# Moving one elementwise sum of a recurrent stage from VectorE to GpSimd, with a new instruction order

## The chip, the cores and the metric

One core of a Trainium2 chip runs the whole program. The time is the device time of one launch in microseconds; of several runs the median counts. The engines of the core that matter here are PE (TensorE, matmuls), ScalarE (ACT), VectorE (DVE) and GpSimd (POOL). Each has its own instruction stream and they meet through semaphores.

## What is computed

The reference is a decoder of twelve blocks on 8192 tokens (128 sequences of 64) of width 128, each block followed by a residual sum and a layer norm. The change lies in the seventh block, a four-layer recurrent block (RWKV). Cut to what matters:

```python
def wkv_scan(k, v, time_decay, time_first):
    w, u = -jnp.exp(time_decay), time_first
    def step(carry, kv):
        num, den, mx = carry
        kt, vt = kv
        max_out = jnp.maximum(mx, kt + u)
        e1, e2 = jnp.exp(mx - max_out), jnp.exp(kt + u - max_out)
        out = (e1 * num + e2 * vt) / (e1 * den + e2)
        ...                                # num, den, mx decayed by w and updated
for l in range(n_layer):                   # 4
    h = layer_norm(x, ln1_w[l]); prev = time_shift(h)
    k, v, r = ...                          # three projections of mixes of h and prev; r through a sigmoid
    x = x + (r * wkv_scan(k, v, time_decay[l], time_first[l])) @ tm_o_w[l].T
    h = layer_norm(x, ln2_w[l]); prev = time_shift(h)
    vv = jnp.square(jax.nn.relu(mix_k(h, prev) @ cm_k_w[l].T)) @ cm_v_w[l].T
    x = x + jax.nn.sigmoid(mix_r(h, prev) @ cm_r_w[l].T) * vv
```

## The kernel before

`rwkv` (from L2121) holds the block. The width of 128 lies on the partitions, tokens along the free axis. The tokens go in 16 tiles of 512 (8 sequences of 64), and each of the four layers passes over the 16 tiles, so there are 64 turns, numbered m. All instructions are written out, and one turn spreads over five to six turn lengths, so that several turns are in work at once. There is one buffer for nearly every intermediate; a step of turn m therefore also waits for the reader of turn m-1.

The steps of a turn are small functions of m, one list for each engine, and each has a due time in the list (in us, on the engine's own scale). `interleaved` (L168; `staggered`, L162, for GpSimd) sorts all steps of all turns by m * 17.9 + due time. The sorted list is the order of the engine's instructions; the due time has no other effect, and an engine runs its list in order, waiting where a semaphore is not yet there. Sixteen end tiles (the block's last layer norm: variance1, end_sum, end_variance2 and their partners) are sorted in behind the last turns with a scale of their own.

The way of a turn, with engines:
- normal1 (VectorE, L2525) makes the first normed tile; half_mixed_k, half_mixed_r (ScalarE) with mix_key, mix_r (VectorE, L2536, L2530) mix it with its shift; keys, values, receptance (PE) project.
- running_max (VectorE, a scan), exponents_ab (two instructions, L2559, L2560), exponent_g (L2568) and clamp_g (L2573) make exponents; exp_ab (L2351) and exp_g (ScalarE) take them. weighted, scan_den (L2586), scan_num (L2593) (VectorE) give the two sums over time, `den` and `num`.
- GpSimd adds the denominator: `dn[1:] = ex0[1:] + den[:-1]` (L2453). VectorE makes `gv = ex0 * v` (bonus, L2601) and then the numerator, in place, `gv[1:] += num[:-1]` (L2606). ScalarE takes the logarithm of the denominator (ln_denominator, L2361); denominator_r (GpSimd, L2458) adds to it ln(1 + exp(-r)), which clamp_r (VectorE) and exp_r, ln_r (ScalarE) have made; reciprocal (ScalarE, L2365) exponentiates, and the quotient (GpSimd, L2463) multiplies it to `gv`. output (PE, L2234) projects.
- residual1 (VectorE, L2610), square2 (ScalarE, L2371), variance2 (PE, L2238), rstd2 (ScalarE), normal2 (GpSimd, L2470) make the second normed tile, mix_k, mix_r2 (VectorE) with half_mixed and half_mixed_r2 (ScalarE) mix it.
- hidden (PE, two halves of 4 matmuls, L2248), rectified (ScalarE, L2399, both halves), squared (first half on ScalarE, L2403; second half on VectorE, L2626), contract (PE, two halves, L2263); receptance2 (PE), clamp_rr (VectorE), exp_rr, ln_rr, sigmoid_rr (ScalarE), gated (VectorE, L2637), centred (PE, L2268), residual2 (VectorE, L2641).

The inputs of bonus, clamp_r, clamp_rr, running_max, exponent_g, exponents_ab's second, weighted, residual1, squared, gated and residual2 include a PSUM bank (`ps`). normal1, mix_key, mix_r, mix_k, mix_r2, clamp_g, exponents_ab's first, scan_den, scan_num and the numerator read SBUF only.

Of the kernel before, what the change touches and what calls it, by code (L numbers as in the profile page):

```python
# [21 lines left out]
ALU = mybir.AluOpType  # L22
# [2098 lines left out]
def rwkv(nc, k, d, ahead=()):  # L2121
# [6 lines left out]
    with ExitStack() as ctx:  # L2128
# [67 lines left out]
        def _(pe):  # L2196
# [88 lines left out]
            def end_variance2(m):  # L2285
# [4 lines left out]
                else:  # L2290
# [1 line left out]
                pe.matmul(ps[:, 4, :], avg[:], rmix[:], start=True, stop=True).then_inc(evar2, 1)  # L2292

            interleaved((0, TURNS, 0, PERIOD, (
                            (1.6, variance1), (24.4, keys), (26.8, values), (32.6, receptance), (45.5, output),
                            (50.4, variance2), (62.5, lambda m: hidden(m, 0)), (60.3, receptance2),
                            (66.3, lambda m: hidden(m, 1)), (71.1, lambda m: contract(m, 0)),
                            (71.2, lambda m: contract(m, 1)), (77.2, centred))),
                        (TURNS, NT, END, END_PERIOD, ((6.3, variance1), (17.8, end_sum), (21.5, end_variance2))))

        @block.scalar
        def _(act):
# [123 lines left out]
            def end_rstd2(m):  # L2426
# [4 lines left out]
                else:  # L2431
# [4 lines left out]
                act.activation(tokens(mm[:]), tokens(mm[:]), ACT.Exp, scale=-0.5).then_inc(ers2, 1)  # L2436

            interleaved((0, TURNS, 0, PERIOD, (
                            (-24.4, square1), (10.7, half_mixed_r), (6.6, half_mixed_k), (-3.5, rstd1), (25.7, exp_r), (27.4, ln_r),
                            (28.2, ln_denominator), (17.3, exp_ab), (17.0, exp_g), (31.8, reciprocal),  # L2440
                            (37.2, square2), (40.3, rstd2), (44.3, half_mixed), (42.7, half_mixed_r2), (52.3, lambda m: rectified(m, 0)), (55.6, squared),
                            (55.8, lambda m: rectified(m, 1)),
                            (57.0, exp_rr), (59.6, ln_rr), (60.1, sigmoid_rr))),
                        (TURNS, NT, END, END_PERIOD, ((-10.7, square1), (-1.6, rstd1), (7.8, end_square2), (13.2, end_rstd2))))

        @block.gpsimd
        def _(pool):
            def denominator(m):
                pool.wait_ge(g_ready, m + 1)
                pool.wait_ge(den_ready, m + 1)  # L2450
                if m:
                    pool.wait_ge(ln_low, m)
                pool.tensor_tensor(flat(dn[:])[:, :, 1:S], ex[:, 0, :, 1:S], den[:, :, 0:S - 1], ALU.add).then_inc(low, 1)  # L2453

            def denominator_r(m):
                pool.wait_ge(ln_low, m + 1)
                pool.wait_ge(er_ready, m + 1)
                pool.tensor_tensor(tokens(dl[:]), er[:], tokens(dl[:]), ALU.add).then_inc(low_r, 1)  # L2458

            def quotient(m):  # L2460
                pool.wait_ge(rec, m + 1)
                pool.wait_ge(top, m + 1)
                pool.tensor_tensor(gv[:], gv[:], tokens(dl[:]), ALU.mult).then_inc(wkv, 1)  # L2463

            def normal2(m):
                pool.wait_ge(rs2, m + 1)
                if m:
                    pool.wait_ge(mixed, m)
                    pool.wait_ge(rmixed2, m)
                pool.tensor_tensor(hp2[:, :, 1:S1], flat(xw[:, at(m)[1]]), flat(rsb[:]), ALU.mult).then_inc(h2, 1)  # L2470

            pool.wait_ge(w_steps, 1)
            staggered(TURNS, PERIOD, (17.6, denominator), (21.7, denominator_r), (32.9, quotient), (38.8, normal2))

        @block.vector
        def _(dve):
# [166 lines left out]
            def end_close(m):  # L2643
# [3 lines left out]
                dve.tensor_tensor(xres[:, e * CT:(e + 1) * CT], ps[:, 2 + e % 2, :], tokens(mm[:]), ALU.mult).then_inc(eclosed, 1)  # L2647

            interleaved((0, TURNS, 0, PERIOD, (
                            (13.0, normal1), (21.7, mix_r), (14.9, mix_key), (31.4, clamp_r), (21.4, running_max), (24.1, exponents_ab),  # L2650
                            (22.4, exponent_g), (22.8, clamp_g), (29.2, weighted), (29.2, scan_den), (29.3, scan_num),
                            (31.1, bonus), (32.0, numerator), (46.5, residual1), (53.1, mix_k), (51.3, mix_r2), (65.6, squared), 
                            (63.2, clamp_rr),
                            (68.4, gated), (72.4, residual2))),
                        (1, NL - 1, PERIOD, PERIOD, ((-16.9, prepare),)),
                        (TURNS, NT, END, END_PERIOD, ((9.8, normal1), (26.1, end_close))))
# [1340 lines left out]
```

## Time and profile before

| | us |
|---|---|
| median of 3 runs | 4742.58 (4739.36 to 4744.38) |
| profiled execution, its own time | 4733.29 |
| its span | 4731.5 |
| of that the recurrent stage, from its first to its last instruction | about 1859 to 2924 |

Over the whole span PE is busy 91%, VectorE 72%, ScalarE 66%, GpSimd 40%. Those shares mix twelve stages with different limits; only the recurrent stage is touched, so it is read alone. Views used: busy time of each engine in a window, and timelines, in which a row is one instruction, or several merged ones, with its start and its duration in us. Durations of instructions that follow one another overlap by up to 0.1 us (0.16 for PE), so the cost of an instruction in a full engine is the distance from its start to the next start. An idle time before an instruction stands in brackets with what ended it.

### The profile page before, as it was taken

The page shows a single profiled execution, that of the slowest core. Times are in us where ns is not written, and L with a number is a line of the kernel's source. Part 1 is how long each engine was busy: PE and PEld are TensorE (multiplying, and loading weights), DVE is VectorE, ACT ScalarE, POOL GpSimd, SP SyncE. Part 2 cuts the span into 40 slices and gives each one's busy share as a digit, 9 for nine tenths or more (in the row PEclk, how much of TensorE's full clock was granted, in tenths as well). Part 3 has the DMA queues.
Part 4 walks back from the last instruction along what each step waited for, and adds up shares of the span by engine and source line. Part 5 has one row for each costly group of instructions (what it writes and reads, how often), then busy time and mean ns, then how long its engine had stood idle before and what let it go on. Part 6 is the DMA issues. An engine that isn't in the chain of part 4 may idle for free. (4 is left out here: it accounts for less than half of the span.)

```text
span 4731.5 us, 101446 instructions
## 1 busy us (share of the span) xinstructions
PE 4322.8 (91%) x37343; PEld 2844.9 (60%) x37343; DVE 3410.2 (72%) x5307; ACT 3131.8 (66%) x5627; POOL 1869.5 (40%) x2204
## 2 busy tenths in 40 slices
PE   8989889899979996999999998789979989999888
PEld 6767556556767774344444444566657767777565
DVE  8978777467764335999999994743359966666748
ACT  6878777466774335899999997742358844444356
POOL 4444344114416771343444430057724412222328
PEclk9999989899989998999999999899989999999999
DMA  3000000000021113000000001211130000000110
GB/s 108 3 2 3 2 1 1 1 1 15 2 61 43 52 52 115 1 1 1 1 1 1 1 1 39 93 40 52 52 100 3 2 2 2 2 2 1 58 56 37
DMA packets 123884, 119.28 MB, mean 25 GB/s; under 512 B 19472, under 2 KB 103952, under 8 KB 122640
## 3 DMA queue, kind: packets, MB, share of 16 engines
q1 hardware_dynamic: 106000, 77.11, 5.3%
q0 software_dynamic: 17408, 35.69, 2.6%
q8 instruction: 315, 5.16, 0.5%
q14 instruction: 161, 1.32, 0.1%
HBM read 82.34 MB, written 30.41 MB: 24 GB/s over the span
## 5 line engine op out<-in xcount | busy, mean ns | idle before, releaser
L1759 POOL DMA_INDIRECT L_ffn_xg<-L_ffn_xrows,L_ffn_take x272 | 264.1, 971 | 282.1 <-DVE L_ffn_take L2054 199.9
L1823 PEld LDWEIGHTS L_ffn_ps<-L_ffn_early_down,L_ffn_mT 128*128 128x128 f32 x1904 | 247.4, 191 | 105.2 <-issue 78.9
L2945 POOL TENSOR_TENSOR L_xattn_E<-L_xattn_E,L_xattn_rz 128x1024 f32<-128x1024 f32 x64 | 123.8, 1935 | 471.7 <-DVE L_xattn_rz L3165 471.7
L1765 POOL DMA_INDIRECT L_ffn_yrows<-L_ffn_yo,L_ffn_put x272 | 269.1, 989 | 99.2 <-issue 55.2
L2453 POOL TENSOR_TENSOR L_attn_dn<-L_attn_ex,L_attn_den 128x504 f32<-128x504 f32 x64 | 130.5, 2040 | 385.4 <-issue 293.0
L1803 PE MATMUL L_ffn_ps<-L_ffn_up,L_ffn_xT 128*128 x544 | 259.6, 559 | 19.8 <-issue 8.3
L1823 PE MATMUL L_ffn_ps<-L_ffn_early_down,L_ffn_mT 128*128 x1904 | 258.9, 276 | 2.4 <-DVE L_ffn_yo L2084 1.3
L2248 PE MATMUL L_attn_ps<-L_attn_mix,L_attn_wck 128*128 128x512 f32 x512 | 243.5, 598 | 0.0
L1913 ACT ACTIVATE L_ffn_mT<-L_ffn_ps 128x512 f32<-128x512 f32 x136 | 81.2, 597 | 236.8 <-PE L_ffn_ps L1812 236.8
L2263 PE MATMUL L_attn_ps<-L_attn_rl,L_attn_wcv 128*128 128x512 f32 x512 | 230.2, 592 | 0.0
L2073 DVE TENSOR_TENSOR L_ffn_m<-L_ffn_b,L_ffn_ps 128x512 f32<-128x512 f32 x136 | 93.6, 688 | 188.3 <-PE L_ffn_ps L1803 188.3
L2069 DVE TENSOR_TENSOR L_ffn_m<-L_ffn_sg,L_ffn_ps 128x352 f32<-128x352 f32 x136 | 70.9, 521 | 213.3 <-ACT L_ffn_sg L1903 213.3
L334 POOL TENSOR_TENSOR L_attn_Kbd<-L_attn_Kt,main_head_of_row 128x1024 f32<-128x1024 f32 x64 | 121.2, 1894 | 253.4 <-issue 244.8
L750 POOL TENSOR_TENSOR L_xattn_Kbd<-L_xattn_Kt,main_head_of_row 128x1024 f32<-128x1024 f32 x64 | 121.2, 1894 | 238.9 <-issue 233.3
L988 DVE TENSOR_REDUCE L_xattn_mx<-L_xattn_ps 128x16 f32<-128x1024 f32 x128 | 156.2, 1220 | 69.9 <-PE L_xattn_ps L812 69.9
L1095 POOL TENSOR_SCALAR L_ffn_aq<-L_ffn_aq,L_ffn_qinv 128x512 f32<-128x512 f32 x64 | 127.0, 1999 | 168.5 <-ACT L_ffn_aq L1245 168.5
L565 DVE TENSOR_TENSOR L_attn_ps<-L_attn_ps,L_attn_bias 128x512 f32<-128x512 f32 x256 | 165.0, 690 | 17.7 <-PE L_attn_ps L398 17.7
L2248 PEld LDWEIGHTS L_attn_ps<-L_attn_mix,L_attn_wck 128*128 128x128 f32 x512 | 92.8, 191 | 130.6 <-issue 130.0
L2263 PEld LDWEIGHTS L_attn_ps<-L_attn_rl,L_attn_wcv 128*128 128x128 f32 x512 | 97.0, 190 | 122.7 <-issue 93.3
L2458 POOL TENSOR_TENSOR L_attn_dl<-L_attn_er,L_attn_dl 128x512 f32<-128x512 f32 x64 | 81.6, 1275 | 209.1 <-ACT L_attn_dl L2361 209.1
L1903 ACT ACTIVATE L_ffn_sg<-L_ffn_ps 128x352 f32<-128x352 f32 x136 | 63.1, 464 | 146.8 <-PE L_ffn_ps L1805 146.8
L824 PE MATMUL L_xattn_ps<-main_ident,L_xattn_E 128*128 128x128 f32 x1024 | 145.5, 281 | 15.5 <-ACT L_xattn_Qt L875 10.3
(619 smaller groups left out, 13439.7 us busy)
## 6 DMA issues: line engine op xcount, KB each, us to landing
L_ffn_row_hot<-L_ffn_yrows SPq DMA_DIRECT2D x32, 256.0 KB, 2.9
L_ffn_col_hot<-L_ffn_yrows SPq DMA_DIRECT2D x32, 256.0 KB, 3.4
L_ffn_w<-in_L_ffn_e_W SPq DMA_DIRECT2D x32, 256.0 KB, 4.7
L_ffn_xrows<-L_ffn_xtok SPq DMA_DIRECT2D x42, 192.0 KB, 2.1
L_ffn_xg<-L_ffn_xrows,L_ffn_take POOLq DMA_INDIRECT x272, 2.5
L_ffn_yrows<-L_ffn_yo,L_ffn_put POOLq DMA_INDIRECT x272, 2.3
main_x<-in_xT SPq DMA_DIRECT2D x8, 512.0 KB, 7.6
main_ctx<-in_ctxT SPq DMA_DIRECT2D x4, 1024.0 KB, 11.5
```

Of the source, the lines that this page charges most:

```text
L565: b = dve.tensor_tensor(scores if in_place else E[t % 2][:, 8 * at:8 * at + 8, :].rearrange("p (a h) k -> p a (h k)", a=2), scores, bias_s ...
L824: m = pe.transpose(to[:, j * P:(j + 1) * P], E[t % 2][:, row:row + 2, :], k["ident"][:])
L988: dve.tensor_reduce(mx[t % 2][:, 16 * half:16 * half + 16], score_rows(half), AX, ALU.max) \
L1095: m = pool.tensor_scalar(aq[u][:, j, :], aq[u][:, j, :], ROUND, qinv[u][:, 1, j:j + 1], ALU.subtract, ALU.mult)
L1759: pool.indirect_dma_start(xg[t % RING][:], None, xrows, bass.IndirectOffsetOnAxis(ap=take[:, t:t + 1], axis=0)) \
L1765: pool.indirect_dma_start(yrows, bass.IndirectOffsetOnAxis(ap=put[:, t:t + 1], axis=0), yo[t % RING][:], None).then_inc(scattered[t % RING ...
L1803: g = pe.matmul(ps[u][:, 0, 0:F], xT[u][:], up[:, bass.ds(at, F)], start=True, stop=True)
L1823: g = pe.matmul(ps[1][:, 3, 0:P], mT[u][0:rows[a], a * P:(a + 1) * P], down[a][:, bass.ds(at, P)], start=(a == 0), stop=(a == FT - 1))
L2248: r = pe.matmul(ps[:, 5 + a % 2, :], wck[:, at(m)[0], a * P:(a + 1) * P], mix[:], start=True, stop=True)
L2263: r = pe.matmul(ps[:, 7, :], wcv[:, at(m)[0], a, :], rl[:, a, :], start=(a == 0), stop=(a == FT - 1))
L2453: pool.tensor_tensor(flat(dn[:])[:, :, 1:S], ex[:, 0, :, 1:S], den[:, :, 0:S - 1], ALU.add).then_inc(low, 1)
L2945: pool.tensor_tensor(E[u][:, j], E[u][:, j], rz[u][:, j].rearrange("p (a o) -> p a o", o=1).to_broadcast([P, 8, P]), ALU.mult).then_inc(no ...
```

## The change

The numerator's sum is taken from VectorE's list and stands as a fifth step in GpSimd's, with the same two waits (for bonus and for scan_num) and the same semaphore at its end, which the quotient and the next turn's scan_num wait for. Beside that every list has new due times: the steps, tiles, buffers and waits are the same, their order on each engine is another.

```diff
 @block.tensor
-  (1.6, variance1), (24.4, keys), (26.8, values), (32.6, receptance), (45.5, output),
-  (50.4, variance2), (62.5, hidden 0), (60.3, receptance2), (66.3, hidden 1), (71.1, contract 0),
-  (71.2, contract 1), (77.2, centred)
-  end: (6.3, variance1), (17.8, end_sum), (21.5, end_variance2)
+  (-4.1, variance1), (15.7, keys), (18.4, values), (22.3, receptance), (39.6, output),
+  (44.8, variance2), (54.9, hidden 0), (54.2, receptance2), (60.2, hidden 1), (63.6, contract 0),
+  (65.1, contract 1), (70.0, centred)
+  end: (-1.7, variance1), (11.9, end_sum), (14.7, end_variance2)
 @block.scalar
-  (-24.4, square1), (10.7, half_mixed_r), (6.6, half_mixed_k), (-3.5, rstd1), (25.7, exp_r), (27.4, ln_r),
-  (28.2, ln_denominator), (17.3, exp_ab), (17.0, exp_g), (31.8, reciprocal), (37.2, square2), (40.3, rstd2),
-  (44.3, half_mixed), (42.7, half_mixed_r2), (52.3, rectified 0), (55.6, squared), (55.8, rectified 1),
-  (57.0, exp_rr), (59.6, ln_rr), (60.1, sigmoid_rr)
+  (-21.7, square1), (13.2, half_mixed_r), (5.9, half_mixed_k), (-6.4, rstd1), (26.1, exp_r), (26.2, ln_r),
+  (24.1, ln_denominator), (16.4, exp_ab), (16.9, exp_g), (30.2, reciprocal), (37.0, square2), (39.2, rstd2),
+  (44.3, half_mixed), (42.1, half_mixed_r2), (52.5, rectified 0), (53.7, squared), (56.8, rectified 1),
+  (56.0, exp_rr), (59.1, ln_rr), (59.9, sigmoid_rr)
   ...
 @block.gpsimd
+def numerator(m):
+    pool.wait_ge(gv_ready, m + 1)
+    pool.wait_ge(num_ready, m + 1)
+    pool.tensor_tensor(flat(gv[:])[:, :, 1:S], flat(gv[:])[:, :, 1:S], num[:, :, 0:S - 1], ALU.add).then_inc(top, 1)
-staggered(TURNS, PERIOD, (17.6, denominator), (21.7, denominator_r), (32.9, quotient), (38.8, normal2))
+staggered(TURNS, PERIOD, (28.1, numerator), (19.2, denominator), (30.1, denominator_r), (34.9, quotient), (39.3, normal2))
 @block.vector
-def numerator(m):
-    dve.wait_ge(gv_ready, m + 1)
-    dve.wait_ge(num_ready, m + 1)
-    dve.tensor_tensor(flat(gv[:])[:, :, 1:S], flat(gv[:])[:, :, 1:S], num[:, :, 0:S - 1], ALU.add).then_inc(top, 1)
-  (13.0, normal1), (21.7, mix_r), (14.9, mix_key), (31.4, clamp_r), (21.4, running_max), (24.1, exponents_ab),
-  (22.4, exponent_g), (22.8, clamp_g), (29.2, weighted), (29.2, scan_den), (29.3, scan_num),
-  (31.1, bonus), (32.0, numerator), (46.5, residual1), (53.1, mix_k), (51.3, mix_r2), (65.6, squared),
-  (63.2, clamp_rr), (68.4, gated), (72.4, residual2)
+  (14.5, normal1), (24.0, mix_r), (15.6, mix_key), (32.7, clamp_r), (21.0, running_max), (22.7, exponents_ab),
+  (23.0, exponent_g), (24.7, clamp_g), (27.7, weighted), (28.8, scan_den), (31.7, scan_num),
+  (33.1, bonus), (46.4, residual1), (57.9, mix_k), (55.5, mix_r2), (67.7, squared),
+  (62.1, clamp_rr), (73.2, gated), (75.7, residual2)
   ...
```

The end groups of ScalarE and VectorE and the due time of prepare (the scaling of a layer's weights, VectorE) move by up to 3.2 as well.

## Rows read from the trace of the kernel before

**Rows 1.** Windows of the stage: busy us of each engine and (instructions).

```profile
core 0: us, PE busy (x) PEld busy (x) DVE busy (x) ACT busy (x) POOL busy (x), PEclk, DMA share, GB/s
...
2240.00:2360.00 120.00, 119.85 (x270) 49.06 (x269) 119.72 (x167) 112.30 (x175) 49.31 (x32) 1.00 0.00 1
```

**Rows 2.** Timeline of VectorE, one turn: start, duration, engine, line, tiles.

```profile
2399.84 1.20 DVE L2593 TENSOR_TENSOR_SCAN L_attn_num<-L_attn_ex,L_attn_bv 128x512 f32<-128x512 f32 x1
2400.96 1.20 DVE L2626 TENSOR_TENSOR L_attn_rl<-L_attn_rl,L_attn_ps 128x1024 f32<-128x1024 f32 x1
2402.07 0.69 DVE L2525 TENSOR_TENSOR L_attn_hp<-L_attn_xw,L_attn_rsa 128x512 f32<-128x512 f32 x1
...
2403.87 0.68 DVE L2606 TENSOR_TENSOR L_attn_gv<-L_attn_gv,L_attn_num 128x504 f32<-128x504 f32 x1
2404.46 0.68 DVE L2637 TENSOR_TENSOR L_attn_er<-L_attn_er,L_attn_ps 128x512 f32<-128x512 f32 x1
...
2409.42 0.73 DVE L2568 SCALAR_TENSOR_TENSOR L_attn_ex<-L_attn_ps,L_attn_col,L_attn_mm 128x504 f32<-128x504 f32 x1
2410.19 0.72 DVE L2573 TENSOR_SCALAR L_attn_ex<-L_attn_ex 128x504 f32<-128x504 f32 x1
2410.84 0.73 DVE L2559 SCALAR_TENSOR_TENSOR L_attn_ex<-L_attn_mm,L_attn_rate 128x504 f32<-128x504 f32 x1
2411.49 0.67 DVE L2560 TENSOR_TENSOR L_attn_ex<-L_attn_ps,L_attn_mm 128x504 f32<-128x504 f32 x1
...
2417.24 0.69 DVE L2525 TENSOR_TENSOR L_attn_hp<-L_attn_xw,L_attn_rsa 128x512 f32<-128x512 f32 x1
```

**Rows 3.** Timeline of PE, the same turn (xN: matmuls merged into one row).

```profile
2400.73 3.60 PE L2263 MATMUL L_attn_ps<-L_attn_rl,L_attn_wcv 128*128 128x512 f32 x8
2404.16 1.02 PE L2201 MATMUL L_attn_ps<-L_attn_sqa,main_avg 128*128 128x512 f32 x2
...
2412.20 1.88 PE L2248 MATMUL L_attn_ps<-L_attn_mix,L_attn_wck 128*128 128x512 f32 x4
```

**Rows 4.** Timeline of ScalarE, the same turn ([idle before, and who ended it]).

```profile
2408.43 0.63 ACT L2365 ACTIVATE L_attn_dl<-L_attn_dl 128x512 f32<-128x512 f32 x1 [0.25 <-POOL L_attn_dl L2458]
...
2412.20 1.04 ACT L2351 ACTIVATE L_attn_ex<-L_attn_ex 128x1008 f32<-128x1008 f32 x1 [0.47 <-DVE L_attn_ex L2560]
...
2414.87 1.00 ACT L2399 ACTIVATE L_attn_rl<-L_attn_ps 128x1024 f32<-128x1024 f32 x1
```

**Rows 5.** Timeline of VectorE, first turns of the stage.

```profile
1878.34 0.42 DVE L2573 TENSOR_SCALAR L_attn_ex<-L_attn_ex 128x504 f32<-128x504 f32 x1
...
1883.97 1.68 DVE L2525 TENSOR_TENSOR L_attn_hp<-main_x,L_attn_rsa 128x512 f32<-128x512 f32 x1
1885.57 0.68 DVE L2601 TENSOR_TENSOR L_attn_gv<-L_attn_ex,L_attn_ps 128x512 f32<-128x512 f32 x1
...
1898.91 1.68 DVE L2525 TENSOR_TENSOR L_attn_hp<-main_x,L_attn_rsa 128x512 f32<-128x512 f32 x1
```

**Rows 6.** Timeline of GpSimd, first turns of the stage.

```profile
1883.12 1.98 POOL L2453 TENSOR_TENSOR L_attn_dn<-L_attn_ex,L_attn_den 128x504 f32<-128x504 f32 x1 [92.36 <-DVE L_attn_den L2586]
...
1900.01 1.71 POOL L2470 TENSOR_TENSOR L_attn_hp<-L_attn_xw,L_attn_rsb 128x512 f32<-128x512 f32 x1
```

**Rows 7.** Timeline of GpSimd, one steady turn.

```profile
2400.06 2.04 POOL L2453 TENSOR_TENSOR L_attn_dn<-L_attn_ex,L_attn_den 128x504 f32<-128x504 f32 x1 [4.59 <-issue]
2402.55 1.35 POOL L2470 TENSOR_TENSOR L_attn_hp<-L_attn_xw,L_attn_rsb 128x512 f32<-128x512 f32 x1 [0.44 <-ACT L_attn_rsb L2379]
2407.13 1.28 POOL L2458 TENSOR_TENSOR L_attn_dl<-L_attn_er,L_attn_dl 128x512 f32<-128x512 f32 x1 [3.23 <-ACT L_attn_dl L2361]
2409.14 1.49 POOL L2463 TENSOR_TENSOR L_attn_gv<-L_attn_gv,L_attn_dl 128x512 f32<-128x512 f32 x1 [0.74 <-ACT L_attn_dl L2365]
```

**Rows 8.** One line's instructions (L2453, the denominator): duration ns min/median/max.

```profile
L2453 POOL TENSOR_TENSOR L_attn_dn<-L_attn_ex,L_attn_den x64: 1980/2042/2048, 1883.1 to 2840.7; 128x504 f32<-128x504 f32 x64
```

**Rows 9.** Timeline of VectorE, its first idle entry after the steady turns.

```profile
2846.75 0.69 DVE L2637 TENSOR_TENSOR L_attn_er<-L_attn_er,L_attn_ps 128x512 f32<-128x512 f32 x1 [1.27 <-PE L_attn_ps L2263]
```

More of the change, by code:

```diff
@@ L2294, in _ @@
             interleaved((0, TURNS, 0, PERIOD, (
-                            (1.6, variance1), (24.4, keys), (26.8, values), (32.6, receptance), (45.5, output),
[L2296 to L2299, printed above, removed]
+                            (-4.1, variance1), (15.7, keys), (18.4, values), (22.3, receptance), (39.6, output),
+                            (44.8, variance2), (54.9, lambda m: hidden(m, 0)), (54.2, receptance2),
+                            (60.2, lambda m: hidden(m, 1)), (63.6, lambda m: contract(m, 0)),
+                            (65.1, lambda m: contract(m, 1)), (70.0, centred))),
+                        (TURNS, NT, END, END_PERIOD, ((-1.7, variance1), (11.9, end_sum), (14.7, end_variance2))))
         @block.scalar
@@ L2438, in _ @@
             interleaved((0, TURNS, 0, PERIOD, (
-                            (-24.4, square1), (10.7, half_mixed_r), (6.6, half_mixed_k), (-3.5, rstd1), (25.7, exp_r), (27.4, ln_r),
[L2440 to L2444, printed above, removed]
+                            (-21.7, square1), (13.2, half_mixed_r), (5.9, half_mixed_k), (-6.4, rstd1), (26.1, exp_r), (26.2, ln_r),
+                            (24.1, ln_denominator), (16.4, exp_ab), (16.9, exp_g), (30.2, reciprocal),
+                            (37.0, square2), (39.2, rstd2), (44.3, half_mixed), (42.1, half_mixed_r2), (52.5, lambda m: rectified(m, 0)), (53.7, squared),
+                            (56.8, lambda m: rectified(m, 1)),
+                            (56.0, exp_rr), (59.1, ln_rr), (59.9, sigmoid_rr))),
+                        (TURNS, NT, END, END_PERIOD, ((-12.6, square1), (-2.2, rstd1), (7.8, end_square2), (12.9, end_rstd2))))
         @block.gpsimd
@@ L2649, in _ @@
             interleaved((0, TURNS, 0, PERIOD, (
-                            (13.0, normal1), (21.7, mix_r), (14.9, mix_key), (31.4, clamp_r), (21.4, running_max), (24.1, exponents_ab),
-                            (22.4, exponent_g), (22.8, clamp_g), (29.2, weighted), (29.2, scan_den), (29.3, scan_num),
-                            (31.1, bonus), (32.0, numerator), (46.5, residual1), (53.1, mix_k), (51.3, mix_r2), (65.6, squared),
[L2653 to L2656, printed above, removed]
+                            (14.5, normal1), (24.0, mix_r), (15.6, mix_key), (32.7, clamp_r), (21.0, running_max), (22.7, exponents_ab),
+                            (23.0, exponent_g), (24.7, clamp_g), (27.7, weighted), (28.8, scan_den), (31.7, scan_num),
+                            (33.1, bonus), (46.4, residual1), (57.9, mix_k), (55.5, mix_r2), (67.7, squared),
+                            (62.1, clamp_rr),
+                            (73.2, gated), (75.7, residual2))),
+                        (1, NL - 1, PERIOD, PERIOD, ((-20.1, prepare),)),
+                        (TURNS, NT, END, END_PERIOD, ((10.2, normal1), (25.1, end_close))))
 def padded_attention(nc, k, d, col, early, ahead):
```

## The prediction, made before the changed kernel was run

> **What bounds the kernel now.** I read the windows by stage first. In the recurrent stage (1859 to 2924 us) VectorE is busy 119.7 of every 120 us, PE 119.85, ScalarE 112.3, GpSimd 49.3 [rows 1]. Busy times of back-to-back instructions overlap a little, so two engines seem full; the timelines tell them apart. VectorE's has no idle entry in a whole turn: each instruction starts when the one before lets it, and a turn, from normal1 to normal1, is 2417.24 - 2402.07 = 15.17 us [rows 2]. PE starts the eight matmuls of contract, back to back, in 2404.16 - 2400.73 = 3.43 us, 0.429 each [rows 3]. A turn has 34 of them (keys, receptance, output, variance1, variance2, receptance2, centred 2 each; values, both halves of hidden, both of contract 4 each; 270 in 120 us = 7.91 turns [rows 1]). So PE needs 34 x 0.429 = 14.59 and is starved for 0.58 a turn. ScalarE idles too, before reciprocal and exp_ab [rows 4]. VectorE sets the pace, and PE stands 0.58 behind it: no change to VectorE can give more than 0.58 a turn.
>
> The third view is GpSimd's timeline beside VectorE's, in the first turns, where they collide. normal1, with two inputs in SBUF, takes 0.69 in the steady turns and 1.68 at 1883.97 and 1898.91 [rows 2, 5], where GpSimd's sum was running [rows 6]: it finished 0.55 after GpSimd's end at 1885.10. GpSimd's normal2 at 1900.01, behind a normal1 that was already waiting, took 1.71, against 1.35 in a steady turn [rows 6, 7]. VectorE's instructions with an input in PSUM (bonus, gated, squared) show no such thing. So a GpSimd instruction and a VectorE instruction that reads only SBUF exclude one another, and who has started finishes first.
> The Trainium skill says this in SBUF — State Buffer, section "Who interferes with whom": the pair of ports is an exclusive lock between GpSimd and a VectorE instruction with two SBUF inputs or in a two-port mode, and issue order decides. By that rule, the trace agrees. It is the rule that speaks against this change, since it moves work onto the engine that blocks VectorE.
>
> **Removed from VectorE.** 64 numerators, each worth 2404.46 - 2403.87 = 0.59 [rows 2]. The new order also parts clamp_g from exponent_g, which it reads: exponent_g takes 0.77 to the next start where the same form at 2410.84 takes 0.65 (the next is at 2411.49), so 0.12 [rows 2]. And clamp_g now overlaps GpSimd's quotient and takes 0.72, where it took 0.42 with GpSimd idle (1878.34) [rows 2, 5, 7]: 0.30 goes if the quotient lies elsewhere. Bare VectorE turn: 15.17 - 0.59 - 0.12 - 0.30 = 14.16.
>
> **Added to GpSimd.** The trace has no numerator there. From below: the denominator's sum, same shape, takes 2.04, but starts at 2400.06 while scan_num (SBUF only, from 2399.84) runs, and squared, the next on VectorE, starts at 2400.96; 0.90 would be waiting and 1.14 work [rows 2, 7]. denominator_r, with 512 contiguous elements, takes 1.28 alone [rows 7]. From above: 2.04, if the denominator's time is all its own. I take 1.14 to 1.28, since three other GpSimd instructions of this size take 1.28 to 1.49. GpSimd then works some 8 of 14.6 us, which it has.
> The Trainium skill, GPSIMD Engine Reference, section "Elementwise — side-by-side cycle accounting", has 2.6 cycles an element for tensor_tensor; an estimate from it at 1.2 GHz is 504 x 2.6 / 1.2 = 1.09 us. By that figure VectorE would wait 0.05 less a turn than by 1.14.
>
> **What it blocks.** Sorting the new due times gives VectorE's turn: gated, mix_r2, running_max, residual2, mix_k, exponents_ab (two), exponent_g, mix_r, clamp_g, clamp_rr, weighted, residual1, scan_den, scan_num, squared, normal1, clamp_r, bonus, mix_key. The numerator waits for bonus, so it comes free while mix_key (SBUF) holds the port, and starts to work when that lets go. gated (PSUM, 0.60) passes; mix_r2 (SBUF) must wait for 1.14 - 0.60 = 0.54 to 1.28 - 0.60 = 0.68, less 0.13, since a blocked instruction has its start-up behind it (the one behind normal1 came at 1885.57, 0.47 after GpSimd's end, not 0.60 [rows 2, 5]). So 0.41 to 0.55 is given back, and VectorE's turn is 14.57 to 14.71. The others fall on PSUM work: the denominator beside squared, as now; normal2 beside clamp_r and bonus; denominator_r beside running_max and residual2; the quotient beside exponents_ab's second and exponent_g.
>
> **The new order.** A turn can't be shorter than any loop of handovers that closes on itself, so I walked the tight ones: a duration plus 0.05 where another engine takes over, 0.429 per matmul, and, inside one engine, a duration less 0.1 on ScalarE (0.53 for 512 elements, 0.90 or 0.94 for 1024) and less 0.09 on VectorE (0.60, scans 1.13) [rows 2 to 4].
> - hidden1, Relu, squared, contract1: 1.88 + 1.00 + 1.20 + 0.15 = 4.23 [rows 2 to 4]; PE's order has 10 matmuls between the two, 4.29. Slack 0.06.
> - hidden0 1.93; on ScalarE Relu 0.90, exp_g 0.52, square 0.95, square2 0.53, exp_rr 0.52, together 3.42; second Relu 1.05; squared 1.25; contract1 and then 16 matmuls to the next hidden0, 6.86: 14.51.
> - squared 1.11, normal1, clamp_r, bonus 1.80, mix_key 0.66, gated 0.60, mix_r2 0.66 and its wait 0.48, running_max 1.13, residual2 0.60, mix_k 0.66, exponents_ab 1.38 with handover, exp_ab 0.95, ScalarE from the first Relu to the second 3.42, Relu 1.05: 14.50.
> - The same through residual1, square2 and variance2: 29.03 for two turns.
> - The quotient: reciprocal follows the second Relu by 7.96 of ScalarE's work and wants 0.71, the quotient 1.9 with its wait, output 4 matmuls before hidden1 (1.72), Relu 1.93: 14.2. The numerator now stands in front of denominator_r and the quotient on GpSimd, and delays neither: denominator_r waits for ln_r, a little later, and has about 0.8 to spare.
> - ScalarE itself: 15.17 less what it idles now, 0.35 before reciprocal, 0.57 before exp_ab and 0.25 behind it (0.25, 0.47 and 0.15 in the view, plus the overlap of 0.1 each time) [rows 4]: 14.0.
>
> None is over 14.6, but five are within 0.1 of it. The longest is VectorE with its port wait, 14.57 to 14.71, beside PE's 14.59. I take 14.66: 0.51 a turn.
>
> **The sum.** The first turns, up to about 1912, are still filling, and VectorE's next idle entry is the 1.27 before 2846.75 [rows 9]: (2845 - 1912) / 15.17 = 61 turns at this pace. 61 x 0.51 = 31 us. The first turns are bound by latency and the drain by PE, with the same matmuls; the new order changes them by a few us either way, and I count 0 and keep 4. The edits to the end group keep its steps' places among the others, and prepare stays behind the same steps: 0. Against the profiled execution: 4733.3 - 31 = 4702. The median of the three runs is 9.3 higher, 4742.6; the same saving gives 4712.
>
> **Rivals.**
> - The order does not close as tightly as it looks on paper: with five loops within 0.1, one more collision (the quotient reaching mix_r or clamp_g, 0.30; a handover of 0.1 to 0.2 for GpSimd, as the 0.22 before the denominator) makes 14.8 to 15.1. For it: the slack of 0.06. Against: such delays fall on different loops and don't add. 14.95 a turn is 13 us: 4729.
> - Slower: the 2.04 of the denominator is GpSimd's own time for a sum over 63 of 64 columns. Then the numerator holds the port for 2.04, mix_r2 waits 2.04 - 0.60 - 0.13 = 1.31, and VectorE's turn is 14.16 + 1.31 = 15.47, 0.30 over now: 61 x 0.30 = 18 us, 4761. It decides from a hold of 1.75 us on. For it: all 64 denominators lie between 1.98 and 2.05 [rows 8]. Against: each has the scan beside it [rows 2, 7], and the other GpSimd sums and products of this size take 1.28 to 1.49 [rows 7].
> - The port goes to a waiting GpSimd instruction between two VectorE instructions that both want it. Then a quotient ready during mix_k goes in front of exponents_ab. It would be ready some 0.2 after that point; if it is early, VectorE loses up to 1.1 in some turns, and about 15.1 on average is no change: 4740.
>
> **How the numbers follow.** Forecast 62%, looser order 20%, GpSimd's own 2.04 12%, lost port 6%. The forecast's own range is a turn of 14.59 to 14.80, with 4 us for the ends: 4704 to 4724. To hold eight in ten I reach over the looser order, to 4738. A difference of 0.2%, 9.5 us, is about what a measurement can tell from none: a turn of 15.01. Forecast and seven tenths of the looser order are faster: 76%. The rest of it and the lost port are the same: 12%. Slower 12%.
>
> **What would show it.** normal1 to normal1 at 14.6 to 14.7; PE in the steady windows without idle; the numerator on GpSimd recorded with 1.5 to 1.7 (port wait and work); mix_r2 on VectorE grown from 0.75 to about 1.2; clamp_g at 0.42. A mix_r2 of 2 us would make the second rival right; idle time on VectorE before squared or weighted, the first; an exponents_ab of over 1.5, the third. The prediction is wrong if the turn is over 15.

## The result and the profile after

| | before | after |
|---|---|---|
| median of 4 runs, us | 4742.9 (4739.4 to 4744.4) | 4708.9 (4706.0 to 4710.0) |
| profiled execution, its own time | 4733.3 | 4708.1 |
| one turn of the recurrent stage | 15.17 | 14.65 |
| recurrent stage | 1066.7 | 1031.9 |

The ratio of the times is 0.993, with an interval of 0.9915 to 0.9942: 34 us less. The forecast was 4712, with 4704 to 4724 as its own range.

Line numbers of after differ by five where the numerator's function moved: normal1 is L2530, mix_key L2541, exponents_ab L2564 and L2565, bonus L2606, clamp_g L2578, and the numerator is L2475, on GpSimd. Rows of other kernels carry that kernel's own numbers; where one counts, it is named.

The window of the same stretch as [rows 1], in the profile of after (busy us of PE, PE's weight loads, VectorE, ScalarE, GpSimd, each with its instructions, then PE's granted clock as a share):

```profile
2240.00:2360.00 120.00, 120.00 (x279) 52.01 (x278) 120.00 (x164) 116.54 (x181) 68.39 (x42) 1.00 0.00 1
```

PE has 279 matmuls in 120 us where it had 270, and no more idle time in the view. VectorE has 164 instructions, fewer than before although more turns pass, and is still full by its busy time. GpSimd has gone from 49.3 to 68.4.

VectorE's timeline over one turn of after, cut to the rows that the prediction spoke of (start, duration):

```profile
2398.68 0.75 DVE L2541 SCALAR_TENSOR_TENSOR L_attn_kmix<-L_attn_hp,L_attn_told,L_attn_kmix 128x512 f32<-128x512 f32 x1
2399.34 0.68 DVE L2637 TENSOR_TENSOR L_attn_er<-L_attn_er,L_attn_ps 128x512 f32<-128x512 f32 x1
2400.01 1.09 DVE L2621 SCALAR_TENSOR_TENSOR L_attn_rmix<-L_attn_hp,L_attn_cold,L_attn_rmix 128x512 f32<-128x512 f32 x1
2401.03 1.21 DVE L2555 TENSOR_TENSOR_SCAN L_attn_mm<-L_attn_decay,L_attn_ps 128x512 f32<-128x512 f32 x1
...
2403.40 0.73 DVE L2564 SCALAR_TENSOR_TENSOR L_attn_ex<-L_attn_mm,L_attn_rate 128x504 f32<-128x504 f32 x1
...
2405.95 0.41 DVE L2578 TENSOR_SCALAR L_attn_ex<-L_attn_ex 128x504 f32<-128x504 f32 x1
...
2409.21 1.20 DVE L2598 TENSOR_TENSOR_SCAN L_attn_num<-L_attn_ex,L_attn_bv 128x512 f32<-128x512 f32 x1
2410.40 1.22 DVE L2626 TENSOR_TENSOR L_attn_rl<-L_attn_rl,L_attn_ps 128x1024 f32<-128x1024 f32 x1
...
2413.33 0.75 DVE L2541 SCALAR_TENSOR_TENSOR L_attn_kmix<-L_attn_hp,L_attn_told,L_attn_kmix 128x512 f32<-128x512 f32 x1
```

mix_key to mix_key is 2413.33 - 2398.68 = 14.65. mix_r2 takes 1.09, which is the wait that was forecast; clamp_g is at 0.41; exponents_ab's first is at its bare 0.73. A small new thing: squared starts 1.19 behind scan_num and not 1.11 or 1.12, and mix_r2 0.67 behind gated and not 0.60. VectorE stands still for 0.08 and 0.07 there, too short for the view to print; mix_r2 waits for ScalarE's half_mixed_r2, squared for the second Relu. So it is no longer quite the engine that sets the pace.

GpSimd's timeline beside it:

```profile
2398.84 1.71 POOL L2475 TENSOR_TENSOR L_attn_gv<-L_attn_gv,L_attn_num 128x504 f32<-128x504 f32 x1
2401.30 1.27 POOL L2458 TENSOR_TENSOR L_attn_dl<-L_attn_er,L_attn_dl 128x512 f32<-128x512 f32 x1 [0.75 <-ACT L_attn_er L2346]
2403.61 1.66 POOL L2463 TENSOR_TENSOR L_attn_gv<-L_attn_gv,L_attn_dl 128x512 f32<-128x512 f32 x1 [1.03 <-ACT L_attn_dl L2365]
```

The numerator is recorded from 2398.84, behind mix_key's start at 2398.68, and waits for its end: 1.71 is wait and work. The quotient comes 0.21 after exponents_ab's first (2403.40) and waits for it, 1.66 in place of about 1.3.

Of the numerator's 64 instances the shortest shows the work alone (in e2 below, where nothing holds it, all 64 take 1.25 to 1.28; the view of one line's instructions: minimum, median, maximum in ns, first and last start):

```profile
L2475 POOL TENSOR_TENSOR L_attn_gv<-L_attn_gv,L_attn_num x64: 1264/1707/1712, 1885.4 to 2809.4; 128x504 f32<-128x504 f32 x64
```

The stage's ends, read the same way: ScalarE's table load at the start (L2303) and the first instruction of the next stage on VectorE (L2812), of before and then of after.

```profile
L2303 ACT ACT_TABLE_LOAD  x1: 1283/1283/1283, 1859.0 to 1859.0; - x1
L2812 DVE CAST L_xattn_lengthf<-L_xattn_early_length x1: 196/196/196, 2925.7 to 2925.7; 128x64 f32<-128x64 int32 x1
```

```profile
L2303 ACT ACT_TABLE_LOAD  x1: 1283/1283/1283, 1858.7 to 1858.7; - x1
L2812 DVE CAST L_xattn_lengthf<-L_xattn_early_length x1: 196/196/196, 2890.6 to 2890.6; 128x64 f32<-128x64 int32 x1
```

1066.7 - 1031.9 = 34.8 us, which covers the whole difference of the medians. Of it 61 turns at 15.17 - 14.65 = 0.52 make 31 to 32; some 3 come from the turns that fill the pipeline (normal1 of the third turn starts at 1916.74 before and 1913.29 after, 3.4 earlier).

The two profiled executions lie only 25.2 apart, because that of before was short by some 10 us in a later stage that the change doesn't touch: one of 16 VectorE instructions there (L3803) takes 10.33 us in after, and none does in the profiled execution of before. First before, then after:

```profile
L3803 DVE TENSOR_TENSOR main_x<-main_x,L_combine_rs x16: 627/1485/1518, 4633.1 to 4726.4; 128x512 f32<-128x512 f32 x16
```

```profile
L3803 DVE TENSOR_TENSOR main_x<-main_x,L_combine_rs x16: 628/875/10332, 4598.9 to 4701.2; 128x512 f32<-128x512 f32 x16
```

That is most likely the 9.3 us between the profiled execution of before and its median: in the profiled executions of all ten kernels below one instruction of this group takes 10.30 to 10.36 us too. What the 10 us are isn't known.

### The profile page after: what moved, and what is told of

Its sections match the earlier page's. It is cut to its first block and busy times, and to the rows that moved or that the text cites. A ratio compares the mean times of both kernels' runs of the same rounds, so it can differ in the third digit from the quotient of the medians.

```text
span 4706.2 us, 101446 instructions
## 1 busy us (share of the span) xinstructions
PE 4295.5 (91%) x37343; PEld 2857.4 (61%) x37343; DVE 3386.1 (72%) x5243; ACT 3132.8 (67%) x5627; POOL 2002.4 (43%) x2268
## 5 line engine op out<-in xcount | busy, mean ns | idle before, releaser
L2453 POOL TENSOR_TENSOR L_attn_dn<-L_attn_ex,L_attn_den 128x504 f32<-128x504 f32 x64 | 130.2, 2034 | 355.9 <-issue 264.9
L586 DVE TENSOR_REDUCE L_attn_mx<-L_attn_ps 128x16 f32<-128x1024 f32 x128 | 156.4, 1222 | 3.3
L3072 ACT ACTIVATE L_xattn_E<-L_xattn_E 128x1024 f32<-128x1024 f32 x64 | 67.6, 1057 | 136.7 <-DVE L_xattn_E L3153 136.7
```

What stands on the lines that cost most here:

```text
L586: dve.tensor_reduce(mx[t % 2][:, 16 * half:16 * half + 16], score_rows(half, t), AX, ALU.max) \
```

## The experiments

All times are medians beside runs of the kernel before on the same chip, whose median was 4740.3 to 4742.3. After and its runs of before in the table were measured apart from these; where an experiment is set beside after, a difference of a few us is better read from the turn in the trace than from the medians.

### Order without the move, and move without the order

```diff
 # e1_order_alone: after, and the numerator back on VectorE, right behind bonus
-staggered(TURNS, PERIOD, (28.1, numerator), (19.2, denominator), ...
+staggered(TURNS, PERIOD, (19.2, denominator), ...
-  (33.1, bonus), (46.4, residual1), ...                # VectorE
+  (33.1, bonus), (33.2, numerator), (46.4, residual1), ...
 # e2_move_alone: before, and the numerator on GpSimd
-  (31.1, bonus), (32.0, numerator), (46.5, residual1), ...    # VectorE
+  (31.1, bonus), (46.5, residual1), ...
-staggered(TURNS, PERIOD, (17.6, denominator), ...
+staggered(TURNS, PERIOD, (21.3, numerator), (17.6, denominator), ...
```

> The new order on all engines, with the numerator kept on VectorE, right behind bonus. Theory (VectorE's own work and the order share the gain): a turn is VectorE's bare 14.16 us plus the numerator's 0.59, so 14.75, with no port wait in front of mix_r2 (0.75 us) and clamp_g at 0.42; 61 turns x 0.42 = 25 us under before, about 4717. Rival (the move carries the gain, the order is only what lets it in): a turn stays at 15.1 to 15.2 and the time within 5 us of before, about 4740.

Measured: 4785.1, ratio 1.0088 (1.0073 to 1.0104), 43 us slower than before; the turn is 15.91. Neither value was near. VectorE's and GpSimd's timelines of this kernel, at exponents_ab (here L2559) and the quotient:

```profile
2399.75 1.75 DVE L2559 SCALAR_TENSOR_TENSOR L_attn_ex<-L_attn_mm,L_attn_rate 128x504 f32<-128x504 f32 x1
```

```profile
2399.61 1.35 POOL L2463 TENSOR_TENSOR L_attn_gv<-L_attn_gv,L_attn_dl 128x512 f32<-128x512 f32 x1 [1.03 <-ACT L_attn_dl L2365]
```

In after the quotient comes 0.21 behind exponents_ab. Here it comes 0.14 ahead of it, and exponents_ab takes 1.75 in place of 0.73, 1.02 a turn. That is the mechanism of the third rival, brought on by the step that was put back.

> The old order, with the numerator moved to GpSimd, between normal2 and denominator_r. Theory (a sum on GpSimd blocks the next SBUF-only instruction of VectorE): bonus ends near 2403.35 in the turn shown of before, GpSimd is free from normal2 at 2403.9, the numerator takes 1.26 to 2405.2, mix_key, now at 2404.46, waits 0.73 less 0.13 of start-up: 0.60 back for the 0.59 removed; a turn of 15.17 and no change, 4743 within 6 us. Rival (VectorE's list alone sets the pace): a turn of 14.6 and 4708, as with the new order.

Measured: 4742.7, ratio 0.9999 (0.999 to 1.0009): no change, as expected, but not for the reason expected. In the steady turns mix_key isn't held up at all. VectorE and GpSimd of this kernel:

```profile
2403.80 0.69 DVE L2637 TENSOR_TENSOR L_attn_er<-L_attn_er,L_attn_ps 128x512 f32<-128x512 f32 x1 [0.47 <-PE L_attn_ps L2263]
2404.41 0.75 DVE L2541 SCALAR_TENSOR_TENSOR L_attn_kmix<-L_attn_hp,L_attn_told,L_attn_kmix 128x512 f32<-128x512 f32 x1
```

```profile
2403.22 1.27 POOL L2475 TENSOR_TENSOR L_attn_gv<-L_attn_gv,L_attn_num 128x504 f32<-128x504 f32 x1
```

gated now waits 0.47 for PE's contract, in the place where the numerator stood: the 0.59 saved turns into a wait. (The numerator runs from 2403.22 beside that wait and beside gated, and ends 0.08 after mix_key's start, too late to lengthen it: 0.75 as ever.)

Why contract comes no earlier is seen further back. The next rows of this kernel, from the timelines of VectorE (residual1), ScalarE (square2), PE's weight loads (variance2), PE (contract) and VectorE (gated), in this order:

```profile
2412.04 0.67 DVE L2610 TENSOR_TENSOR L_attn_xw<-L_attn_xw,L_attn_ps 128x512 f32<-128x512 f32 x1
2412.74 0.63 ACT L2371 ACTIVATE L_attn_sqb<-L_attn_xw 128x512 f32<-128x512 f32 x1
2413.42 0.30 PEld L2238 LDWEIGHTS L_attn_ps<-L_attn_sqb,main_avg 128*128 128x128 f32 x2 [0.83 <-ACT L_attn_sqb L2371]
2415.24 3.60 PE L2263 MATMUL L_attn_ps<-L_attn_rl,L_attn_wcv 128*128 128x512 f32 x8
2418.95 0.69 DVE L2637 TENSOR_TENSOR L_attn_er<-L_attn_er,L_attn_ps 128x512 f32<-128x512 f32 x1 [0.47 <-PE L_attn_ps L2263]
```

From gated (2403.80) VectorE works without a gap to residual1, 8.24; square2 starts 0.70 later, variance2 0.68 later, contract 1.82 and the next gated 3.71 later: 15.15. This loop closes on itself and doesn't hold the numerator, which stood in front of gated. Over the steady turns it gives 15.14, against the 15.17 of before: in the old order VectorE was full, but a second loop lay only 0.03 under it, and an instruction taken from VectorE outside that loop could bring no more than this. The new order has to open that loop before the move can pay.

Of these two kernels neither gains: with the order alone the time rises by 43, with the move alone it stays, with both it falls by 34. That the order needs the move isn't shown by this; the next two sections put the numerator elsewhere.

### How near is the quotient's turn at the port?

e1 says that after works because the quotient comes 0.21 behind exponents_ab. The place of reciprocal on ScalarE sets when the quotient can start, so it can be moved alone.

```diff
 # e5_reciprocal_later: e1_order_alone, and
 # e6_reciprocal_earlier: after, and
-  (30.2, reciprocal)
+  (31.2, reciprocal)    # e5: one step later on ScalarE
+  (29.3, reciprocal)    # e6: one step earlier
```

> The changed kernel with one swap on ScalarE the other way: reciprocal in front of rstd1, so that it starts as soon as denominator_r has ended, and the quotient comes free about 0.3 earlier. Theory (in the changed kernel the quotient comes free 0.21 after exponents_ab's first has started, and a waiting GpSimd instruction goes in front of a VectorE one that isn't running yet): the order at the port turns over, exponents_ab's first grows from 0.73 to about 1.75, VectorE's turn goes to 14.50 + 1.0 = 15.5, and the time to 4755 to 4770, slower than before, by an instruction that was made to come earlier. Rival (such a wait is short, or is taken up by VectorE's slack): turn 14.65 and 4709.

Measured: 4761.1, ratio 1.004 (1.0025 to 1.0056), 52 us slower than after for one step of ScalarE moved; the turn is 15.57, 0.92 more, and 61 x 0.92 = 56. VectorE and GpSimd of this kernel (exponents_ab is L2564 again):

```profile
2403.10 1.75 DVE L2564 SCALAR_TENSOR_TENSOR L_attn_ex<-L_attn_mm,L_attn_rate 128x504 f32<-128x504 f32 x1
```

```profile
2403.02 1.29 POOL L2463 TENSOR_TENSOR L_attn_gv<-L_attn_gv,L_attn_dl 128x512 f32<-128x512 f32 x1 [0.74 <-ACT L_attn_dl L2365]
```

The quotient starts 0.08 ahead and keeps the port for its whole length. This reproduces e1's port loss by another edit, and shows that after's 0.21 us is a narrow margin.

> The kernel of the new order with the numerator on VectorE, with one swap on ScalarE: reciprocal behind half_mixed_r instead of in front of it, so that the quotient comes 0.6 us later. Theory (that kernel is slow because the quotient comes free 0.14 before exponents_ab's first and takes the port in front of it): the quotient now comes free while exponents_ab's first runs, waits for it and works beside its second, which reads PSUM; exponents_ab's first falls from 1.75 to 0.73, a turn from 15.91 to 14.75 to 14.9, the time from 4785 to 4716 to 4726. Rival (something else in the new order needs the numerator off VectorE): the turn stays at 15.9, the time at 4785.

Measured: 4745.4, ratio 1.0006 (0.9997 to 1.0016). exponents_ab's first is back at 0.74, the turn falls from 15.91 to 15.25, 40 us less: the port part is right. But the result isn't near 4720 as expected; 0.6 a turn remains. PE of this kernel:

```profile
2408.06 1.12 PE L2215 MATMUL L_attn_ps<-L_attn_kmix,L_attn_now 128*128 128x512 f32 x2 [0.33 <-DVE L_attn_kmix L2536]
```

PE waits for mix_key before keys. From hidden1's start (2400.63) to keys is 7.43 here, through Relu, squared, normal1, clamp_r, bonus, the numerator and mix_key; behind it PE has 18 matmuls to the next hidden1, 7.72, and the first instruction after a wait costs it 0.10 more: 15.25. The numerator in front of mix_key lies on that loop. That is the second thing that the move takes away from this order.

### Is it the place or the engine?

```diff
 # e9_numerator_behind_gated: after with reciprocal at 31.2 and the numerator on VectorE
-  (33.1, bonus), (46.4, residual1), ...
+  (33.1, bonus), (37.5, numerator), (46.4, residual1), ...    # sorts behind mix_key and gated
```

> The new order with reciprocal behind half_mixed_r and the numerator on VectorE, now behind mix_key and gated instead of in front of mix_key. Theory (a numerator in front of mix_key lengthens the loop hidden, Relu, squared, mix_key, keys, hidden to 15.25; VectorE's own work is only 14.75): the keys wait no more, a turn of 14.75 to 14.85, 4715 to 4721, so that the move to GpSimd is worth 0.1 to 0.2 a turn over a VectorE numerator in its best place. Rival (VectorE can't carry the numerator anywhere in this order): a turn of 15.1 or more, 4738 or more.

Measured: 4714.7, ratio 0.9944 (0.9929 to 0.9959), as expected; the turn goes between 14.72 and 14.80, 14.77 on average. VectorE of this kernel:

```profile
2403.66 0.68 DVE L2637 TENSOR_TENSOR L_attn_er<-L_attn_er,L_attn_ps 128x512 f32<-128x512 f32 x1
2404.26 0.68 DVE L2606 TENSOR_TENSOR L_attn_gv<-L_attn_gv,L_attn_num 128x504 f32<-128x504 f32 x1
2404.85 0.75 DVE L2621 SCALAR_TENSOR_TENSOR L_attn_rmix<-L_attn_hp,L_attn_cold,L_attn_rmix 128x512 f32<-128x512 f32 x1
```

The numerator costs VectorE 0.59 and mix_r2 is back at 0.75. On GpSimd it costs VectorE nothing itself and mix_r2 0.34. Beside its own runs of before, the new order with a well-placed numerator on VectorE gets 26 us (4740.3 to 4714.7) of the 34; the move to GpSimd adds some 8. The intervals of the two ratios overlap, so the medians alone don't tell them apart. The traces do: the stage takes 1039.8 us here and 1031.9 in after, and the turns, 14.77 and 14.65, differ by 0.12, 61 x 0.12 = 7. (This kernel differs from after by the place of reciprocal too; how much of the 8 is due to that wasn't run.) So three quarters of the gain is the order's, once the numerator stands well in it.

### What holds the turn at 14.65?

By the prediction it is VectorE with mix_r2's wait. By the small waits in VectorE's timeline it is another loop. Taking the numerator away removes the port wait and 1.26 us of GpSimd's work, and nothing on PE or ScalarE.

```diff
 # e4_no_numerator: after without the sum
-staggered(TURNS, PERIOD, (28.1, numerator), (19.2, denominator), ...
+staggered(TURNS, PERIOD, (19.2, denominator), ...
-    pool.wait_ge(top, m + 1)        # quotient
+    pool.wait_ge(gv_ready, m + 1)
-    if m: dve.wait_ge(top, m)       # scan_num
```

> The changed kernel without the numerator: the sum over earlier tokens is left out of the quotient, on every engine. Theory (PE and its handover loop bind): mix_r2 falls from 1.09 to 0.75 us and VectorE gains 0.35 of idle time, and the turn stays at 14.65. Rival (VectorE with its port wait binds): the turn falls to PE's 14.59.

Measured: the turn is 14.65 (2413.51 - 2398.86, mix_key to mix_key), unchanged; 60 turns, from the first squared to the 61st, take 879.2 us in both kernels. VectorE of this kernel:

```profile
2400.19 0.75 DVE L2614 SCALAR_TENSOR_TENSOR L_attn_rmix<-L_attn_hp,L_attn_cold,L_attn_rmix 128x512 f32<-128x512 f32 x1
...
2410.58 1.22 DVE L2619 TENSOR_TENSOR L_attn_rl<-L_attn_rl,L_attn_ps 128x1024 f32<-128x1024 f32 x1 [0.25 <-ACT L_attn_rl L2399]
```

mix_r2's wait is gone, and VectorE stands still for as much before squared. The wait costs nothing in after. (The one run took 4702.9. Of its 6 us less none lies in those turns: the stage starts 2.9 later and reaches its first squared in 2.7 less, and the rest lies behind the stage; one run doesn't say why.)

What binds is seen in after's timelines of PE, ScalarE, VectorE (shown above) and PE's weight loads, in this order:

```profile
2407.42 1.88 PE L2248 MATMUL L_attn_ps<-L_attn_mix,L_attn_wck 128*128 128x512 f32 x4
2409.14 1.02 PE L2238 MATMUL L_attn_ps<-L_attn_sqb,main_avg 128*128 128x512 f32 x2
2410.00 3.66 PE L2263 MATMUL L_attn_ps<-L_attn_rl,L_attn_wcv 128*128 128x512 f32 x8
2413.49 1.02 PE L2201 MATMUL L_attn_ps<-L_attn_sqa,main_avg 128*128 128x512 f32 x2
```

```profile
2409.34 1.02 ACT L2399 ACTIVATE L_attn_rl<-L_attn_ps 128x1024 f32<-128x1024 f32 x1
```

```profile
2411.67 0.30 PEld L2263 LDWEIGHTS L_attn_ps<-L_attn_rl,L_attn_wcv 128*128 128x128 f32 x2 [0.62 <-DVE L_attn_rl L2626]
```

hidden1 starts at 2407.42, Relu 1.92 later, squared 1.06 later (2410.40), contract1's first weights 1.27 later (2411.67), its first matmul 0.10 later, four matmuls before 2413.49: 4.35 in all. The 10 matmuls in PE's order between the two take 4.29. contract lasts 3.49 for 3.43. So the loop is PE's 14.59 and 0.06: 14.65, in after and without the numerator alike.

### Can the last 0.06 be had?

With variance1 between the halves of contract, contract1 comes 0.86 later and the wait should go.

```diff
 # e3_variance1_between: after, and
-  (-4.1, variance1), ... (65.1, contract 1)
+  (-7.2, variance1), ... (65.1, contract 1)
```

> The changed kernel with variance1 moved on PE from behind both halves of contract to between them, so that 12 matmuls instead of 10 stand between hidden's second half and contract's second half. Theory (the turn of 14.65 is PE's 14.59 plus 0.06 in which contract's second half waits for hidden, Relu and squared): the wait goes, a turn is 14.59 to 14.60, 61 x 0.06 = 4 us under the changed kernel, about 4705. Rival (VectorE with its wait for the port is the bound at 14.65): the same turn of 14.65 and 4709.

Measured: 4719.3, ratio 0.9949 (0.9936 to 0.9963), 10 us slower than after, with a turn of 14.85. The wait before contract1 is gone. But contract1 ends later, and gated waits for it; behind gated PE waits with centred. VectorE and PE of this kernel:

```profile
2407.78 0.69 DVE L2637 TENSOR_TENSOR L_attn_er<-L_attn_er,L_attn_ps 128x512 f32<-128x512 f32 x1 [0.48 <-PE L_attn_ps L2263]
```

```profile
2407.51 1.02 PE L2215 MATMUL L_attn_ps<-L_attn_kmix,L_attn_now 128*128 128x512 f32 x2
2408.53 1.13 PE L2268 MATMUL L_attn_ps<-L_attn_er,main_center 128*128 128x512 f32 x2
2409.49 1.02 PE L2204 MATMUL L_attn_ps<-L_attn_hp,L_attn_now 128*128 128x512 f32 x2
```

centred starts 1.02 after keys and not 0.86, and the step after it 0.96 later: 0.26 given back for 0.06 won, 0.20 a turn, 61 x 0.20 = 12.

The next three move centred back: values is split into its two pairs of matmuls, and one pair goes behind centred. The first two missed. (The last of the three texts calls e8_values_split_early the first kernel.)

```diff
 # e7_values_split: e3_variance1_between, and
-    mixed_in(3, 1, at(m)[0]).then_inc(v_mm, 1)          # values, 4 matmuls
+    pe.matmul(ps[:, 3, :], now[...], hp1[:, :, 1:S1], start=True, stop=False)
+def values_old(m):
+    pe.matmul(ps[:, 3, :], old[...], hp1[:, :, 0:S], start=False, stop=True).then_inc(v_mm, 1)
-  (18.4, values), (70.0, centred)
+  (18.4, values), (18.5, values_old), (72.15, centred)
 # e8_values_split_early: the same with (72.12, centred), (54.24, receptance2)
 # e10_split_and_reciprocal: e8 with (31.2, reciprocal)
```

> The changed kernel with variance1 between the halves of contract and, new, centred between the two pairs of matmuls of values, so that 12 matmuls stand from hidden's second half to contract's second half, and 8 instead of 6 from there to centred. Theory (the changed kernel's turn is PE's 14.59 plus 0.06 of waiting in front of contract's second half, and moving variance1 alone only put a wait of 0.26 in front of centred instead): both waits go, a turn of 14.59 to 14.65, 4705 to 4709. Rival (VectorE's way from contract over gated to exponents_ab and exp_ab binds whatever PE does, or the quotient, free only 0.06 after exponents_ab's first here, comes in front of it): 14.85 and 4719, or over 15.5 and over 4755.

Measured: 4821.5, ratio 1.0169 (1.0156 to 1.0183), turn 16.50. centred had sorted behind receptance2, two matmuls later than meant; residual2 waits 0.95 for it, and the quotient then meets mix_k, which takes 1.54.

> The changed kernel with variance1 between the halves of contract and centred behind the first two matmuls of values, in front of receptance2 (in the run before this one it had come behind receptance2, 0.86 later, and residual2 waited 0.95 for it). Theory (the changed kernel is bound by PE's 34 matmuls and 0.06 of waiting in a handover): no wait of PE is left, a turn of 14.59 to 14.66, 4705 to 4709. Rival 1 (the way from contract over gated and exponents_ab to exp_ab and the first Relu binds, 14.85 as with variance1 moved alone): 4719. Rival 2 (the quotient, free only 0.06 after exponents_ab's first, comes in front of it or of mix_k): a turn of 15.5 or more, over 4755.

Measured: 4780.0, ratio 1.008 (1.0067 to 1.0094), turn 15.84. VectorE and GpSimd of this kernel:

```profile
2409.76 1.79 DVE L2563 SCALAR_TENSOR_TENSOR L_attn_ex<-L_attn_mm,L_attn_rate 128x504 f32<-128x504 f32 x1
```

```profile
2409.74 1.27 POOL L2462 TENSOR_TENSOR L_attn_gv<-L_attn_gv,L_attn_dl 128x512 f32<-128x512 f32 x1 [1.02 <-ACT L_attn_dl L2364]
```

The quotient comes 0.02 ahead and takes the port: VectorE's order hadn't changed, the phase between the engines had.

> The first kernel of this call with reciprocal behind half_mixed_r as well, so that the quotient comes free 0.6 later, well inside exponents_ab's first. Theory: the same turn as the first, 14.59 to 14.66, without the risk at the port, or 0.1 more if output then waits for the quotient: 4705 to 4715. Rival (the quotient's end, 0.2 later, is on the path): mix_r waits for it and output comes late, 14.8 and 4717.

Measured: 4720.0, ratio 0.9954 (0.994 to 0.9968), turn 14.79. The port loss is gone (exponents_ab 0.73), 1.05 a turn. What remains are gaps on PE, 0.06 behind output and 0.11 behind variance2 among them: near the rival's 14.8 and 4717. Which of two loops ends last here, the one through the quotient or the one through gated and exponents_ab, isn't settled. Apart from the one that leaves out the sum, no kernel was measured faster than after. So the last 0.06 wasn't had, and that PE's 14.59 can be reached isn't shown.

## Why the prediction was right, and where not

- **The pace and its floor.** VectorE set the pace, with PE's bare work 0.58 behind: right. What the prediction didn't see is a second loop of the old order, over residual1, square2, variance2, contract and gated, only 0.03 behind (e2). The forecast doesn't suffer, since it was made by walking the loops of the new order. The turn fell by 0.52, 14.65 measured for 14.66.
- **What VectorE sheds.** The numerator's 0.59, clamp_g back to 0.41, exponent_g apart from its reader: right. VectorE's turn less its two small waits is 14.50 (14.65 - 0.08 - 0.07), which is the 14.16 of the prediction and a port wait of 0.34; the prediction had 14.57 to 14.71.
- **The numerator on GpSimd.** Work of 1.264, inside 1.14 to 1.28, and 1.71 recorded, at the top of the "1.5 to 1.7". The second rival (2.04 is the sum's own time) is out. The Trainium skill, GPSIMD Engine Reference, section "Elementwise — side-by-side cycle accounting", gave 1.09 by estimate; the measurement decides, 0.17 more.
- **mix_r2's wait.** 0.34 (1.09 for 0.75) where 0.41 to 0.55 was forecast; by the prediction's own formula the measured work gives 1.264 - 0.60 - 0.13 = 0.53. mix_r2 started 0.67 behind gated and not 0.60, as it also does without the numerator (e4), so 0.07 of the hold was over already. And the numerator ended 1.12 behind mix_key's end (2400.55 - 2399.43), 0.14 sooner than 1.264: a GpSimd instruction that was made to wait has its start-up behind it too, which the prediction granted to VectorE alone.
- **The step that failed: "the longest is VectorE with its port wait".** Without the wait the turn stays at 14.65 (e4). The loop hidden1, Relu, squared, contract1 was put at 4.23 with a slack of 0.06; it measures 4.35, and is 0.06 too long. Its durations were right within 0.04 (1.88 + 1.02 + 1.22 = 4.12 for 4.08); the handovers were 0.23 and not 0.15, since into PE the weights come first: 0.05 to their load and 0.10 more to the matmul. So one term was 0.16 too long (VectorE's way, 14.50 for the 14.66 taken) and another 0.12 too short (this loop, 4.35 for 4.23), and the longest came out at 14.65 all the same. That the number is right to 0.01 is luck; that the turn lies close above PE's 14.59 is not, since PE's work was right and no loop walked came out much over it.
- **Quotient beside exponents_ab.** Put beside its second and exponent_g; it arrives 0.21 behind the first and waits for it. The third rival had "ready some 0.2 after that point" as its measure. That was exact, and e6 and e8 show that the condition is the sharp one the rival stated: 0.08 or 0.02 too early costs exponents_ab 1.02 to 1.06, in every turn that was looked at and not in some, which gives 4761 and not the rival's 4740. Its price was too small.
- **The ends.** Counted as 0 with 4 kept in the range; they gave 3 us, and the median is 3 below the forecast.
- **Not asked in the prediction:** what each part does alone. The first experiment was expected at 4717, or 4740 by its rival, and came at 4785, 45 us off or more: only the loops with the numerator on GpSimd had been walked, not those with it still on VectorE.

## What to carry to other kernels

A move off the full engine pays only as far as the next loop lets it: here 0.59 left VectorE, and with the old order nothing came of it, since a loop that doesn't hold the numerator was only 0.03 shorter. A full engine isn't proof that it is the only bound. Most of the gain, 26 of 34 us, could be had without the move, by the order and the right place for the numerator. Where GpSimd and VectorE share a port, look not at who has how much work but at who comes first at each meeting, and by how much; a meeting decided by 0.2 us is worth 1 us a turn, and any edit anywhere that shifts the phase can turn it. When walking loops, give each handover the price of its receiving engine, PE's with the weight load.

## What the runs showed of the chip

- **Who comes first keeps the port, to some hundredths of a us.** A GpSimd product that was recorded 0.02, 0.08 and 0.14 us ahead of a VectorE instruction on SBUF made that one take 1.79, 1.75 and 1.75 (e8, e6, e1); 0.06, 0.21 and 0.48 behind it (e3, after, e5), 0.74, 0.73 and 0.74. Over the turns of all kernels in which the two met, the quotient was recorded 0.01 to 0.16 ahead of exponents_ab 184 times, and each time exponents_ab took 1.74 or more; 0.04 to 0.7 behind it 370 times, and it never did; at 0.03 behind it went once either way (e10, 1.84; e5, 0.74). The Trainium skill says in SBUF — State Buffer, section "Who interferes with whom", that issue order decides; the traces agree but for those 0.03 us, with the loser waiting the winner's whole length.
- **A scan with its inputs in SBUF holds the port too.** GpSimd's sum takes 1.26 alone and 1.71 behind mix_key, while the denominator's, of the same shape, takes 2.04 when it starts beside scan_num [rows 2, 7, 8]. That fits a wait for the scan. No run was made for it, but one turn of after tells the two readings apart: there the denominator starts 0.50 behind scan_num and not 0.21.

```profile
2218.70 1.20 DVE L2598 TENSOR_TENSOR_SCAN L_attn_num<-L_attn_ex,L_attn_bv 128x512 f32<-128x512 f32 x1
2219.20 1.76 POOL L2453 TENSOR_TENSOR L_attn_dn<-L_attn_ex,L_attn_den 128x504 f32<-128x504 f32 x1 [4.44 <-issue]
```

It takes 1.76 and not 2.04, and ends 2.26 behind scan_num's start, as in all 64 turns of after (2.25 or 2.26). The end stays with the scan, wherever the sum starts, so the 2.04 isn't the sum's own time. Six more of the kernels have one such turn, with 1.75 or 1.76.

- **A wait of PE can cost more than its length.** The step after a wait starts 0.96 behind the one that waited and not 0.86: centred in e3, which waited 0.16, and keys in e5, which waited 0.50. The shortest wait, 0.05 in front of contract1 in after, shows no such addition (contract 3.49 for 3.43).
